# A two-layer graph attention kernel: the second pair's x loaded right behind the first value weights, and the splits of the later weights moved to other places in the first steps

## What is computed

```python
# layer 0
q, k = src @ Wq + bq, src @ Wk + bk
attn = softmax(q @ k.T / sqrt(dh))
out = sum((attn * (adj == r)) @ (src @ Wv[r] + bv[r]) for r in range(4))
x = ln(src + out @ Wo + bo, g1, beta1)
x = ln(x + gelu(x @ W1 + b1) @ W2 + b2, g2, beta2)          # 256 -> 1024 -> 256
# layer 1
e = leaky_relu(q1 @ k1.T); attn = softmax(where(adj > 0, e, -9e15))
h = layernorm(attn @ v1, g1, b1)
out = layernorm(concat([h, x]) @ Wffn.T, g2, b2) + x
```

## Time and profile before

| what | value |
|---|---|
| median of 3 runs | 2392.83 us (2391.24 to 2400.36) |
| the profiled execution, own time | 2393.2 us |
| its span | 2390.2 us |
| busy in the span | PE 96%, PEld 77%, DVE 88%, ACT 89%, POOL 72% |
| mean granted clock of TensorE | 0.984 of full speed |
| HBM | 40.12 MB read, 16.78 MB written |
| first of the 40 slices (60 us each): PE, ACT, POOL | 3, 4, 5 tenths busy |
| other slices, PE | 8 or 9 tenths and more, until the last |

### The profile page before, as it was taken

The page is one execution under the profiler, slowest core; times in us unless marked ns, Lnnn a source line. Parts: engine busy times, 40 slices in busy tenths (PEclk is TensorE's granted clock), DMA queues, the critical chain, the costliest instruction groups (busy, mean ns, idle before and its releaser), DMA issues. The chain is left out here.

```text
span 2390.2 us, 80704 instructions
## 1 busy us (share of the span) xinstructions
PE 2282.8 (96%) x30272; PEld 1849.5 (77%) x30272; DVE 2108.4 (88%) x3979; ACT 2118.1 (89%) x5963; POOL 1718.8 (72%) x1879
## 2 busy tenths in 40 slices
PE   3899999999999999999999999999999999999984
PEld 2678778788788788788887877877877878888863
DVE  4789989999999998999999998998998999999963
ACT  4699989999999999999999999999999999999973
POOL 5467767777777777777777777777776777777763
PEclk7999999999999999999999999999999999999997
DMA  6456756756756756756666765675675675685653
GB/s 166 85 92 115 134 104 120 133 112 113 142 107 113 138 108 112 138 108 116 134 117 108 133 123 107 128 129 105 124 129 108 121 142 104 114 141 107 110 94 67
DMA packets 950372, 280.83 MB, mean 117 GB/s; under 512 B 879073, under 2 KB 949473, under 8 KB 949986
## 3 DMA queue, kind: packets, MB, share of 16 engines
q1 hardware_dynamic: 948128, 275.42, 62.6%
q10 hardware_dynamic: 1858, 0.27, 0.1%
HBM read 40.12 MB, written 16.78 MB: 24 GB/s over the span
## 5 line engine op out<-in xcount | busy, mean ns | idle before, releaser
L970 DVE TENSOR_TENSOR pm<-pT,bank 128x4096 f16<-128x4096 f16 x256 | 573.5, 2280 | 8.3 <-DMA pT<-p0h 8.2
L470 PE MATMUL bank<-wv,xT 128*128 128x512 f16 (+1 forms) x2304 | 450.5, 346 | 0.0
L766 ACT ACTIVATE bank<-bank,p_nmax 128x128 f32<-128x128 f32 x1024 | 356.9, 371 | 28.8 <-DVE p_nmax L956 25.3
L470 PEld LDWEIGHTS bank<-wv,xT 128*128 128x128 f16 x2304 | 221.0, 98 | 179.0 <-issue 19.3
L1200 POOL TENSOR_TENSOR h<-h_f,h 128x512 f16<-128x512 f32 (+1 forms) x257 | 294.6, 1167 | 88.5 <-ACT h L740 88.3
L470 PE MATMUL bank<-yT,w 128*128 128x256 f16 x3072 | 356.9, 273 | 0.0
L470 PE MATMUL bank<-w,h 128*128 128x256 f16 x3072 | 345.6, 272 | 2.7 <-POOL h L1200 2.7
L1200 POOL TENSOR_TENSOR x_rows<-x,x_rows 128x512 f16<-128x512 f32 x128 | 148.2, 1158 | 270.4 <-ACT x_rows L809 157.8
L755 ACT ACTIVATE p<-p,p_nmax 128x128 f32<-128x128 f32 x1024 | 337.0, 436 | 0.8
L470 PEld LDWEIGHTS bank<-yT,w 128*128 128x128 f16 x3072 | 295.5, 98 | 41.2
L470 PEld LDWEIGHTS bank<-w,h 128*128 128x128 f16 x3072 | 295.9, 98 | 36.2 <-issue 2.8
(11 more groups left out here) (107 smaller groups left out, 4859.9 us busy)
## 6 DMA issues: line engine op xcount, KB each, us to landing
x_sb<-in_x_dram SPq DMA_DIRECT2D x64, 256.0 KB, 3.0
adj_i<-in_adj_dram SPq DMA_DIRECT2D x128, 128.0 KB, 2.8
out_dram<-x2b SPq DMA_DIRECT2D x64, 256.0 KB, 2.9
xT<-x_rows SPq DMA_TRANSPOSE x128, 3.2
pT<-p0h SPq DMA_TRANSPOSE x128, 4.6
oT<-o_rows SPq DMA_TRANSPOSE x128, 3.2
pT<-p1h SPq DMA_TRANSPOSE x128, 5.0
pm<-in_L_gnn_Wv_dram SPq DMA_DIRECT2D x4, 256.0 KB, 6.3
```

The source lines that it names most:

```text
L470: last = nc.tensor.matmul(o, l, r, start=(first and k == 0), stop=(final and k == len(todo) - 1))
L766: last = nc.scalar.activation(ps(f"s0_{r}")[:, at:at + P], ps(f"s0_{r}")[:, at:at + P], ACT.Exp, bias=p0_nmax[:, r, g, c:c + 1], accum_out ...
L970: V_.tensor_tensor(pm0[g][:, s], pT0[g][:, s].unsqueeze(1).broadcast_to([P, REL, HEADS, P]), edges[:, g].unsqueeze(2).broadcast_to([P, REL ...
```

## The change

It moves x of pair 1 to SP's load right behind wv0; issues the loads of w1 and w2 from ACT, inside `x_high(0)`; moves wo0 from the first parts to the later ones (after w1 and w2, staged in another buffer, low half now by POOL); splits w1 and w2's high halves on ACT behind the evacuation of k0 of pair 0, and the other four at the old place; on POOL runs, behind `x_low(1)`, the low halves of w1 and w2, then `fold_gain`, then the other four low halves; and issues the transposition of wffn in the step of pair 0's second probability transposition instead of ahead of SP's steps. PE's waits count the new order.

```diff
         at = place("wk0", stage0, at, KC, D)
-        at = place("wo0", stage0, at, KC, D)
         at = place("wv0", stage0, at, KC, V)
+        at = place("wo0", x2[X2R - 1][:].rearrange("p g d -> p (g d)"), 0, KC, D)
...
-        first_parts = [("wq0", wq0), ("wk0", wk0), ("wv0", wv0), ("wo0", wo0)]
-        later_parts = [("w1", w1), ("w2", w2), ("wq1", wq1), ("wk1", wk1), ("wv1", wv1)]
+        first_parts = [("wq0", wq0), ("wk0", wk0), ("wv0", wv0)]
+        later_parts = [("w1", w1), ("w2", w2), ("wo0", wo0), ("wq1", wq1), ("wk1", wk1), ("wv1", wv1)]
...
                         sp.dma_start_transpose(w_bias[:].rearrange("p (o j) -> p o j", o=KC), shift_rows).then_inc(s_wffn, 16)
+                        sp.wait_ge(s_fold, 4)
+                        sp.dma_start_transpose(wffn[:].rearrange("p s c (o j) -> p (s c o) j", o=KC),
+                                               ffn_rows.rearrange("p s c o j -> p (s c o j)")).then_inc(s_wffn, 16)
...
                                  ).then_inc(landed_w["wv0"], 16)
+                rows_from_x(1)
                 sp.wait_ge(S["xT0_lo"], 1)
...
-                load_weight(sp, "wo0")
                 load_weight(sp, "wffn")
                 sp.dma_start(b1_row1, row(a["L1_gnn_b1"])).then_inc(s_ends, 16)
                 sp.dma_start(g1_row1, row(a["L1_gnn_g1"])).then_inc(s_ends, 16)
-                rows_from_x(1)
-                for name in ("w1", "w2", "wq1", "wk1", "wv1"):
+                for name in ("wo0", "wq1", "wk1", "wv1"):
                     load_weight(sp, name)
                 for tile, v in late_rows:
                     sp.dma_start(tile[:], row(a[v])).then_inc(s_rows, 16)
-                sp.wait_ge(s_fold, 4)
-                sp.dma_start_transpose(wffn[:].rearrange("p s c (o j) -> p (s c o) j", o=KC),
-                                       ffn_rows.rearrange("p s c o j -> p (s c o j)")).then_inc(s_wffn, 16)
                 pipeline(steps)
...
                 def first_weights_high():
+                    load_weight(act, "w1")
+                    load_weight(act, "w2")
...
                     last.then_inc(S[name + "_sb"], 1)
+                    if m == 0 and name == "k0":
+                        later_weights_high(later_parts[0:2])
...
                     if m == 0 and r == ROWS - 1:
-                        later_weights_high()
+                        later_weights_high(later_parts[2:])
...
-                    if m == 0:
-                        fold_gain()
...
                     if m == 1:
-                        later_weights_low()
+                        later_weights_low(0, 2)
+                        fold_gain()
+                        later_weights_low(2, 6)
```

More of the change, by code:

```diff
@@ L582, in output_projection @@
                     if m == 0:
-                        pe.wait_ge(s_lo0, 4)
+                        pe.wait_ge(s_lo1, 3)
                     for g in range(G):
@@ L610, in queries_keys_1 @@
                     if m == 0:
-                        pe.wait_ge(s_lo1, 3 if job == "q1" else 4)
+                        pe.wait_ge(s_lo1, 4 if job == "q1" else 5)
                     for c in range(KC):
@@ L620, in values_1 @@
                     if m == 0:
-                        pe.wait_ge(s_lo1, 5)
+                        pe.wait_ge(s_lo1, 6)
                     for g in range(G):
@@ L705, in first_weights_high, with later_weights_high @@
                         nc.scalar.activation(tile[:, 0], staged[name], copy).then_inc(s_hi0, 1)
-                def later_weights_high():
-                    for name, tile in later_parts:
+                def later_weights_high(parts):
+                    for name, tile in parts:
                         act.wait_ge(landed_w[name], count_w[name])
@@ L744, in leaky_1 @@
                     if m == 0:
-                        act.wait_ge(s_lo1, 5)
+                        act.wait_ge(s_lo1, 6)
                     if past(m):
@@ L1212, in fold_gain, with later_weights_low @@
                     low(ffn_rows[:, 1], by_column, ffn_rows[:, 0]).then_inc(s_fold, 1)
-                def later_weights_low():
-                    for n, (name, tile) in enumerate(later_parts):
-                        pool.wait_ge(s_hi1, n + 1)
+                def later_weights_low(first, end):
+                    for n, (name, tile) in enumerate(later_parts[first:end]):
+                        pool.wait_ge(s_hi1, first + n + 1)
                         low(tile[:, 1], staged[name], tile[:, 0]).then_inc(s_lo1, 1)
```

## The result

| | before | after |
|---|---|---|
| median of 17 runs each | 2392.83 us (2389.86 to 2403.21) | 2387.53 us (2384.71 to 2391.71) |
| the profiled execution, own time | 2393.2 | 2386.67 |
| its span | 2390.2 | 2384.8 |
| mean granted clock | 0.984 | 0.988 |

The ratio of after to before is 0.9977, with a 95% interval of 0.9968 to 0.9986. By that ratio the change makes the kernel 5.5 us faster (3.3 to 7.7); the two medians lie 5.3 apart. I had forecast 2380.5, or 12.4 faster. The time lies in my range and on the side that I named, and within the 0.5% to which I had given 0.52, but the gain is less than half of the forecast.

What follows compares the result with a forecast made beforehand. PE, busy 990 of 1000 us, bounds the steady part, so only the pipeline's start can move: 10.6 - 2.4 - 0.7 + 3.1 + 1.8 = 12.4 us sooner, giving 2380.5 us, range 2376 to 2389.

Steps and rivals of the forecast that it cites:

- Term 1: ACT's waits for wo0 and x of pair 1 go; scores at 17.03 instead of 27.63, a gain of 10.6 us.
- Term 2: First transposition lands later, behind x of pair 1 and beside w1 and w2; q0 at 14.1, a cost of 2.4 us.
- upper bound: Transposition's delay if the two DMA queues take turns from about 8 us: q0 at 16.1, a cost of 4.4 us.
- at half of 0.28 MB per us: Rate assumed for SP's queue while sharing with ACT's; at 0.14, the 0.42 MB left at 10 us takes 3.0 us.
- other rivals: Only the chain's head moves, 2385.3 us (chance 0.15); x not brought forward, 2385.4 (0.03); w2 starves, slower (0.04).
- Term 3: High halves of w1 and w2 on ACT ahead of the first exponential; a cost of 0.7 us.
- the condition that w2 has landed: w2 through at 16 to 19 us, before ACT splits it, with 2 us to spare.
- Terms 4 and 5: Fewer high halves ahead of ACT's values, 3.1 us sooner; DVE's two small fold operations wait less for POOL, gaining 1.8.
- The bound of 0: No gain on DVE's two small fold operations if POOL's subtraction for w2 still runs there.
- Terms 6 and 7: PE is ready for the head products with 0.3 us to spare; wffn's transposition and other moved work cost nothing.
- The sum: Start of the pipeline: 10.6 - 2.4 - 0.7 + 3.1 + 1.8 = 12.4 us sooner.
- turns from 8 us: Rival: queues alternate from 8 us, the transposition's delay costs 4.4 instead of 2.4; 10.4 us gained, 2382.4; chance 0.17.

Runs made afterwards that it cites:

- experiment 1: Changed kernel with w1 and w2 issued on ACT only behind the first transposition of x; ratio to the kernel before 0.9944, 2382.44 us.
- experiment 4: Changed kernel with w1 and w2 loaded by SP and all six high halves split at the old places, POOL folding first; ratio to before 0.9956.
- Experiment 7: On top of experiment 1, POOL's fold ahead of w1's and w2's low halves; one trace, time not used, masked products 2.2 us later than in experiment 1.
- Experiment 8: On top of experiment 1, wffn's transposition back at its old place ahead of SP's steps; ratio to the kernel before 0.9967.

## Why the prediction was right and wrong

**Term 1, the two waits: right.** 10.6 less the transposition's delay of 8.2 is 2.4, and the scores came 2.26 sooner. In the first experiment, where that delay is 0.95, they came 8.7 sooner and not 9.65, since k0's products took 2.77 instead of 1.80, at full granted clock; why stays open. (The parts of this term as written put the scores at 17.05, not 17.03, which moves nothing.)

**Term 2 is the step that failed.** I priced the first transposition's delay at 2.4, between 0.9 and an "upper bound" of 4.4; it was 8.2 (19.92 against 11.70). The moment at which the turns begin was a small part of it: w1's packets set in at about 9 us (ACT's queue moved 0.22 MB from 9 to 10), between the 8 and the 10 that I had weighed, and by my own arithmetic that is worth 1.0. x by itself was right, 0.9 against 0.95 in experiment 1, but beside the loads it costs 2.0. Wrong was "at half of 0.28 MB per us": I split the bytes in half. The rows from 12 to 16 us show the packets split in half, 492 to 495, and SP's are the small ones. So nearly all of w1 and w2 passed ahead of the transposition: ACT's queue moved 2.09 MB from 8 to 20 us, and at the 0.28 MB per us that both queues together made on average there, that is 7.5, against 7.3 measured between experiment 1 and the changed kernel. The agreement is one of averages, since the pace within went from 0.38 to 0.16. The page "DMA: Bandwidth & Descriptors" of the Trainium skill, in its section on queues, rings and completion order, does say that the turns are by packet; I had read it as an equal share. The equal counts between the large loads and SP's queue agree with that, but the page has one packet hold several descriptors, which the profile's counts can't tell apart, and the 576 to 176 beside the bias columns do not show one for one. My upper bound was therefore no bound, and the range held the time only because of the room for other rivals.

**Term 3, w1 and w2 split ahead of the exponential: right in number, by luck in part.** 0.7 forecast; the lead went from 2.26 to 1.79, so 0.5. But from the scores to the first exponential it is 3.35 in the changed kernel and 1.96 in experiment 4, without the splits, so they cost 1.4 there; 0.9 of it was hidden, because the scores took 1.17 instead of the 2.09 of before, which the sum did not foresee. And the condition that w2 has landed held only because everything was late: it landed at 21.4, not at 16 to 19, and by the forecast ACT would have asked for it at 21.1. In experiment 1, where it is issued later, ACT waits 1.41 for it.

**Terms 4 and 5: right, a little low.** 3.1 and 1.8 forecast. The first value row of DVE leads by 4.87 (38.96 against 43.83), 3.1 more than the first exponential; the two small operations took 1.67 instead of 3.96, a gain of 2.3. Experiment 7 shows the cause of the second. The bound of 0, w2's subtraction still running there, did not come about in the changed kernel. The page "SBUF — State Buffer" of the Trainium skill states in "Who interferes with whom" that a DVE instruction with two inputs in SBUF waits for a running GpSimd one that reads there; 3.98 beside 4.05 agrees. The cast has one input only; that it waits too is read off its end, 48.15 beside 48.12 before and 37.64 beside 37.62 in experiment 4.

**Terms 6 and 7: right.** PE had q0 and k0 of pair 1 at 48.23 (46.31 plus 1.92) and began the head products at 48.38, 4.57 behind the start of the masked products, as before (50.97 and 55.54). wffn's transposition was issued at 46.87 and held SP for 1.99, not 6.45; the attention's came at 58.81, 7.3 sooner. Experiment 8 shows what its move is for.

**The sum.** With 8.2, 0.5 and 2.3 in place of 2.4, 0.7 and 1.8 it is 7.3, and the masked products led by 7.2. In experiment 1, where term 2 is 0.95, the forecast's sum would be 13.9; the masked products led by 12.5 and the kernel took 13.4 us less than before. Of the rivals the first, "turns from 8 us", named the right place and was too cheap by half.

## What to carry to other kernels

That a load goes into another engine's queue does not make it free for what waits in the path's own queue. Beside the loads of w1 and w2 the two queues moved as many packets each, and the transposition with its small packets was left a quarter of the bytes. Issue bulk loads only when what the start of the chain waits for has landed, and count packets, not bytes, when pricing what lies beside a short DMA. And when a change bundles several moves, price each against the others: here one moved line gave as much as the whole, and the rest was worth 5 us only with the loads put right.

## What the runs showed of the hardware that I had not expected

- Two DMA queues that both held large work moved as many packets each: 492 and 495 in 4 us, with 0.22 and 0.63 MB. The same transposition took 12.4 from issue to landing, 8.0 and 8.1 beside one of the loads, 5.1 with x alone ahead of it and 4.1 before.
- A DMA issue on ACT does not wait for the activations ahead of it: w1 was issued at 3.64, while the table load ran, and the activation ahead of it in the program started at 5.60.
- The same transposition can hold SP for very different times: that of wffn took 6.45 before, 1.99 after and 2.03 in experiment 8. Before, the queue still moved 0.33 MB in the us after its issue; in experiment 8 it had moved nothing for over 1 us. That the backlog is the cause is likely, but no run varies it alone.
- The scores of pair 0 took 2.09 before, at a granted clock of 0.50 (PE had been idle for 11.6 us), and 1.17 after, at 1.00, where it had been idle for 1.02. It gained nothing, as ACT was busy with the weights.
